# Edges of the passes in a four-layer graph kernel: split last loads, moved fills and table loads, another order at the end

## Chip, cores and metric

The kernel runs on one core of one Trainium2 chip. The metric is device time in microseconds (us) of one execution; the profile comes from one execution, and other executions were timed as well.

## What is computed

A graph of 3327 nodes with 64 features has a sparse weighted adjacency matrix `adj` (3327 x 3327, float32). Four layers follow each other, each with a residual and a normalisation:

```python
x = _layernorm(x + _L0_gnn_ref(x, adj, L0_gnn_W), axis=-1)
x = _layernorm(x + _L1_gnn_ref(L1_gnn_t, x, adj), axis=-1)
x = _layernorm(x + _L2_gnn_ref(x, adj, L2_gnn_weight, L2_gnn_bias), axis=-1)
x = _layernorm(x + _L3_gnn_ref(x, L3_gnn_W, ..., adj), axis=-1)
```

Layer 0 is two hops, `x = tanh([adj @ x, x] @ W[k])`. Layer 1 needs one product `adj @ x`. Layer 2 weights each row's neighbours by powers of 0.5 of their rank. Layer 3 runs twice what follows (H is `adj`):

```python
edge_feat = H.T @ V
att = jax.nn.softmax(Q @ edge_feat.T * scale * H, axis=1)
att_scores = att.mean(axis=0)
importance = 0.5 * structural + 0.5 * att_scores
comp_mask = jax.nn.softmax(importance / TAU) >= th_comp
cos = xn @ xn.T
edge_mask = (jax.nn.softmax(cos * H / TAU, axis=1) >= th_edge) & comp_mask[:, None]
H_pruned = H * edge_mask
...
agg = (H_pruned.T * dv_isqrt) @ transformed * de_inv[:, None]
msg = (dv_isqrt[:, None] * (H_pruned @ agg)) @ Theta
return jax.nn.relu(msg)
```

## The kernel before, in words

The matrix is padded to 3328 = 26 blocks of 128 rows (`NB` is 26, `NP` 3328, `HALF` 1664, `BANK` 512). A block is one load of 128 x 3328 float32 (1664 KB); the matrix doesn't fit on the chip, so each of 15 passes over it streams blocks from memory: `hop0`, `hop1`, `ode` (the first two layers), `decay0`, `decay1` (the third), and twice `edge`, `att`, `cos`, `down`, `up` (the fourth layer; the digit behind a name is the repetition `it`). All loads are issued by SP in one order written out by hand; each waits until the block that used its slot before is done (`block_done`).

The streams of the engines are also written by hand. What the change and the prediction touch:

- **hop, edge, down, up** (`aggregate`, `gather`): for a block, TensorE multiplies 64 feature columns by the block's two halves in chunks of 512, 512, 512 and 128 columns, into four banks of PSUM. The block's matmuls start when the whole block has landed (`landed`). In `down` and `up` VectorE first masks the block in place; it masks the last block of `up` in two parts (L1693), columns 0 to 1024 of each half and then the rest.
- **start**: SP loads the constants and the early weights (`early_constants`, L481 and L482) between the second and third block of `hop0`. After `hop0` the parts of its result are copied from PSUM (L1064 on ScalarE, L1289 on VectorE) and multiplied by those weights in `early_fold`.
- **att, cos** (`product`): TensorE makes the block of products in four pieces, VectorE multiplies each by the block of H and takes the maximum (L1480), ScalarE takes the exponential (L1188), and TensorE adds up columns with `columns(k)`, two blocks later. In `att` VectorE makes the reciprocal of the row sum (`weigh`, L1582), and for the last block multiplies it by `real`, which is 0 for the one row past 3327 (L1586). In `cos` GpSimd computes the cut of each row (`cut_of`, L608), ScalarE marks what lies below it (`sign`, L1204), VectorE prunes (L1637; the last two blocks L1642) and GpSimd prunes a share of the columns (`prune_share`, L618 and L621).
- **between the passes of layer 3**: the column sums are copied from PSUM (L1198 and L1591 after `att`, L1224 after `cos`) and turned by transposes (`turn_sums`, L933). Two softmaxes over the nodes use all-reduces of GpSimd (`node_softmax`, L626 and L628; L636 and L642 are all-reduces whose result isn't used).
- **fills**: `keep_running(n)` issues n matmuls on zeros, 512 columns each, whose result isn't used.
- **end**: after `up1` the result is folded in three parts of 8, 8 and 10 blocks of 64 columns (0, 1, 2). `kept_part`, `var_of` and `inverse_of` on VectorE, squares and roots on ScalarE, make the normalisation. ScalarE scales parts 0 and 1 a block at a time (L1264, L1270), VectorE part 2 (L1763). SP stores parts 0, 1 and 2 in that order (L572).

## Time and profile before

| what | value |
|---|---|
| timed executions, median of 3 | 1688.93 us (1687.36 to 1691.55) |
| the profiled execution, its own time | 1691.28 us |
| its span, first to last instruction | 1689.3 us |
| PE busy | 1468.6 us, 87% |
| DVE busy | 1140.3 us, 67% |
| ACT busy | 731.2 us, 43% |
| POOL busy | 348.9 us, 21% |
| DMA, mean over the span | 342 GB/s |
| chain that ended last | PE 55%, DMA 17%, DVE 16%, issue 8%, ACT 3% |

PE is TensorE's matmuls, PEld its weight loads, DVE VectorE, ACT ScalarE, POOL GpSimd, SP the queue that issues the loads. The chain that ended last is followed back from the last instruction, at each step to what released it; "issue" is time in which the engine waited for nothing that the profile shows. The clock that the profile gives is the one granted to TensorE, as a share of 2.4 GHz. A row of a timeline has the start, the duration, the engine, the line, the operation, out<-in and the count, and in brackets how long the engine had been idle and what ended that.

### The profile page before, as it was taken

Reading aid. Unit: us, or ns where it says so; the run is one execution under the profiler, and the core shown is the slowest. Engines: PE = TensorE matmul, PEld = TensorE weight load, DVE = VectorE, ACT = ScalarE, POOL = GpSimd, SP = SyncE. Lnnn points to the kernel's source line nnn. Section 1 sums busy time; section 2 is a strip of 40 time slices with the busy share of each in tenths; the row PEclk is TensorE's granted clock in tenths of the full one; section 3 lists DMA queues with packets and bytes.
Section 4 is the critical chain, followed back from the end, with each engine's and each line's share of the span. In section 5 each row is a group of like instructions: output and inputs, shape, how many; then the busy total and the mean of one; then the engine's idle time right before and its main releaser. Section 6 shows DMA issues by size and latency. Waiting matters only on the chain.

```text
span 1689.3 us, 24305 instructions
## 1 busy us (share of the span) xinstructions
PE 1468.6 (87%) x10171; PEld 632.4 (37%) x10171; DVE 1140.3 (67%) x1616; ACT 731.2 (43%) x671; POOL 348.9 (21%) x303
## 2 busy tenths in 40 slices
PE   6789999999999998676788799998996777798895
PEld 2234434434444343233332344443443333333442
DVE  0000213677612997899989798216996999989896
ACT  0000101533311775999930242113775999800433
POOL 0000000000000894444400000002992444200000
PEclk9999999999999999899999999999999999899998
DMA  9979598799799996466689999999993766699994
GB/s 401 427 297 403 220 425 335 259 319 410 303 423 383 427 425 268 167 247 247 231 332 428 419 417 426 425 426 421 413 407 119 256 243 243 243 406 427 426 424 176
DMA packets 60620, 578.41 MB, mean 342 GB/s; under 512 B 6240, under 2 KB 6496, under 8 KB 20832
## 3 DMA queue, kind: packets, MB, share of 16 engines
q1 hardware_dynamic: 60512, 576.87, 84.7%
q8 instruction: 80, 1.31, 0.3%
q14 instruction: 28, 0.23, 0.0%
HBM read 575.14 MB, written 1.70 MB: 341 GB/s over the span
## 4 chain that ended last, share of the span: by engine, by line
PE 55%; DMA 17%; DVE 16%; issue 8%; ACT 3%; SPq 0%; DVEq 0%; POOL 0%; ACTq 0%; POOLq 0%
PE ps L654 53%; DMA arena<-adj_t 8%; DMA slot<-adj 6%; DVE shared L1480 4%; DVE slot L1673 4%; DVE slot L1696 2%; DMA shared<-adj_t 2%; DVE shared L1673 2%; DMA slot<-adj_t 2%; PE ps L1008 1%; DVE shared L1696 1%; ACT shared L1234 1%; ACT shared L1188 1%; DVE slot L1637 1%; DVE slot L1642 0%
## 5 line engine op out<-in xcount | busy, mean ns | idle before, releaser
L654 PE MATMUL ps<-shared 64*128 64x416 f32 (+3 forms) x1292 | 279.4, 473 | 102.7 <-DVE max L1480 100.1
L1480 DVE CUSTOM_DVE_ANT_1 shared<-ps,slot 128x832 f32<-128x832 f32 x352 | 342.0, 1021 | 5.1 <-PE ps L654 2.5
L1188 ACT ACTIVATE shared<-shared,negmax 128x3327 f32<-128x3327 f32 x88 | 270.0, 3069 | 67.7 <-DVE negmax L1491 65.1
L654 PE MATMUL ps<-slot,cur 128*64 128x512 f32 (+1 forms) x1440 | 262.9, 516 | 16.8 <-DVE slot L1673 14.8
L593 POOL TENSOR_SCALAR cur<-shared,row_rz 128x768 f32<-128x768 f32 x32 | 70.5, 2204 | 870.7 <-DVE row_rz L1582 865.9
L654 PE MATMUL ps<-arena 64*128 64x416 f32 (+1 forms) x1072 | 208.2, 525 | 1.0 <-DMA arena<-adj 0.5
L654 PEld LDWEIGHTS ps<-shared 64*128 64x128 f32 (+2 forms) x1292 | 113.5, 162 | 235.7 <-DVE max L1480 145.5
L1234 ACT ACTIVATE shared<-ps 128x2048 int16<-128x2048 int16 (+1 forms) x52 | 78.1, 1554 | 279.5 <-PE ps L1008 279.5
L654 PEld LDWEIGHTS ps<-slot,cur 128*64 128x64 f32 x1440 | 96.7, 137 | 179.4 <-issue 154.7
L1204 ACT ACTIVATE arena<-shared,cut 128x3328 fp8e4<-128x3328 f32 x52 | 159.1, 3059 | 8.7 <-POOL cut L608 7.5
L1637 DVE SCALAR_TENSOR_TENSOR slot<-arena,slot 128x2752 f32<-128x2752 int8 x48 | 145.0, 3021 | 12.4 <-ACT arena L1204 12.4
L654 PE MATMUL ps<-shared,cur 128*64 128x512 f32 (+1 forms) x672 | 125.7, 522 | 15.1 <-DVE shared L1673 7.5
L1289 DVE COPY shared<-ps 128x512 f32<-128x512 f32 x3 | 2.1, 692 | 193.5 <-PE ps L654 193.5
L654 PEld LDWEIGHTS ps<-arena 64*128 64x128 f32 (+1 forms) x1072 | 87.6, 175 | 108.5 <-issue 69.5
L1696 DVE SCALAR_TENSOR_TENSOR slot<-shared,slot 128x3328 f32<-128x3328 int8 x32 | 114.5, 3620 | 10.7 <-ACT shared L1234 8.5
L654 PE MATMUL ps<-slot,ones 128*32 128x128 f32 (+3 forms) x1456 | 102.2, 408 | 10.3 <-DVE slot L1642 10.3
L654 PE MATMUL ps<-shared,arena 128*64 128x320 bf16 (+4 forms) x798 | 105.5, 361 | 0.4 <-DMA shared<-adj 0.4
L654 PE MATMUL ps<-slot,arena 128*64 128x512 f32 x496 | 91.0, 515 | 5.0 <-DMA slot<-adj 5.0
L1130 ACT ACTIVATE shared<-ps 128x512 int16<-128x512 f32 x104 | 53.6, 517 | 88.6 <-PE ps L654 88.3
L1064 ACT ACTIVATE shared<-ps 128x640 f32<-128x640 f32 (+1 forms) x6 | 3.9, 650 | 198.7 <-PE ps L654 198.7
L1673 DVE SCALAR_TENSOR_TENSOR slot<-arena,slot 128x3328 f32<-128x3328 int8 x24 | 85.9, 3621 | 3.0 <-DMA slot<-adj 3.0
L618 POOL TENSOR_SCALAR share_marks<-shared,cut 128x576 bf16<-128x576 f32 x48 | 82.4, 1717 | 4.7
(203 smaller groups left out, 1590.8 us busy)
## 6 DMA issues: line engine op xcount, KB each, us to landing
slot<-adj SPq DMA_DIRECT2D x159, 1664.0 KB, 9.5
slot<-adj_t SPq DMA_DIRECT2D x62, 1664.0 KB, 14.2
arena<-adj_t SPq DMA_DIRECT2D x26, 1664.0 KB, 23.9
arena<-adj_t SPq DMA_DIRECT2D x52, 832.0 KB, 7.2
shared<-adj SPq DMA_DIRECT2D x26, 1664.0 KB, 14.6
shared<-adj_t SPq DMA_DIRECT2D x22, 1664.0 KB, 15.0
arena<-adj SPq DMA_DIRECT2D x15, 1664.0 KB, 15.3
xw<-x_nodes SPq DMA_DIRECT2D x1, 832.0 KB, 4.5
```

Of the source, the lines that this page charges most:

```text
L593: weighted = pool.tensor_scalar(halves(dst), product, row_rz[:, k % 3:k % 3 + 1], None, ALU.mult)
L618: pool.tensor_scalar(marks, product, cut[:, k % 2:k % 2 + 1], None, ALU.is_ge)\
L654: return pe.matmul(o, l, r, start=start, stop=stop, skip_group_check=True)
L1008: last = pe.transpose(ps[:, 4 * BANK + q * D:4 * BANK + (q + 1) * D].bitcast(BF16), sign_pairs[:, q * HALF + pair * P:q * HALF + (pair + 1 ...
L1130: act.activation(dst, bank(c, w), ACT.Relu).then_inc(relu_act, 1)
L1188: act.activation(bufs[b][:, 0:N], bufs[b][:, 0:N], ACT.Exp, bias=negmax[:, b:b + 1], accum_out=rowsum[:, b:b + 1]).then_inc(exp_done, 1)
L1204: act.activation(interleaved(sign_marks[:, row * NP:(row + 1) * NP]), halves(prod[k % 2][:, 0:NP]), ACT.Sign, bias=cut[:, k % 2:k % 2 + 1] ...
L1234: act.activation(turned[pair % 2][:, cols], ps[:, 4 * BANK:4 * BANK + HALF].bitcast(I16)[:, cols], ACT.Copy)\
L1480: dve.tensor_tensor_reduce(out=pieces3(bufs[k % len(bufs)], c), in0=pieces_psum(piece_place(name, k, c)[0]), in1=pieces3(slot_of(name, k), ...
L1637: dve.scalar_tensor_tensor(out=own, in0=marks, scalar=0.0, in1=own, op0=ALU.is_le, op1=ALU.mult, accum_out=conn).then_inc(pruned, 1)
L1673: dve.scalar_tensor_tensor(out=slot, in0=interleaved(signs[:, row * NP:(row + 1) * NP]), scalar=0.0, in1=slot, op0=ALU.is_le, op1=ALU.mult ...
L1696: dve.scalar_tensor_tensor(out=slot, in0=marks, scalar=0.0, in1=slot, op0=ALU.is_le, op1=ALU.mult).then_inc(up_pruned, 1)
```

## The change

It has seven parts.

1. The early weights are loaded behind the last block of `hop0` instead of ahead of its third, under a semaphore of their own. VectorE's scaling of `decay_w` moves behind its copy of `hop0`'s result.
2. The last blocks of `hop0`, `edge0`, `up0`, `edge1` and `up1` are loaded in two parts. For `hop0` these are columns 512 to 1664 of each half, then 0 to 512; for the others 0 to 1024, then the rest. TensorE (`hop0`, `edge`) or VectorE (`up`) starts on the first part.
3. GpSimd runs a one-element `tensor_scalar` right behind the softmax that follows `att`.
4. The last block of `att` is summed over 127 rows of the 128, so the multiplication by `real` goes. Its sums of the first bank are made first; ScalarE copies them and TensorE turns them while those of the second bank are made and copied.
5. Ahead of `cos`'s last `columns` there are 8 fills.
6. ScalarE takes a square root that isn't used, behind its copy of `cos`'s sums.
7. At the end the order changes: part 2 is centred later, its squares are taken before part 0 is scaled, parts 1 and 2 are both scaled by VectorE, and SP stores parts 1, 2, 0.

```diff
@@ sync
+                    if name == "hop0" and k == NB - 1:
+                        for cols, signal in ((slice(BANK, HALF), first_landed), (slice(0, BANK), loaded)):
+                            sp.dma_start(halves(slot[:, :])[:, :, cols], halves(adj_t[row * P:(row + 1) * P, :])[:, :, cols])\
+                                .then_inc(signal, 16)
...
+                    if name in SPLIT_LOADS and k == NB - 1:
+                        whole = halves(source[row * P:(row + 1) * P, :])
+                        for cols, signal in ((slice(0, 2 * BANK), first_landed), (slice(2 * BANK, HALF), loaded)):
+                            sp.dma_start(halves(slot[:, :])[:, :, cols], whole[:, :, cols]).then_inc(signal, 16)
...
             early_stream("hop0")
+            sp.dma_start(early_wt, early_weights).then_inc(weights_loaded, 16)
             late_constants()
...
-            for c in range(3):
-                sp.wait_ge(out_ready, PARTS[c].stop if c < 2 else PARTS[1].stop + 1)
+            for c in (1, 2, 0):
+                if c == 0:
+                    sp.wait_ge(out_ready, PARTS[0].stop)
+                else:
+                    sp.wait_ge(ends_scaled, c)
@@ gpsimd
                 node_softmax(2 * it)
+                pool.tensor_scalar(tiny["unused_step"][:, :], ones32[:, 0:1], 1.0, None, ALU.mult).then_inc(steps_ready, 1)
@@ tensor
             def gather(name, k, source, slot):
...
+                    elif name.startswith("edge") and k == NB - 1 and o == 2 * BANK:
+                        landed(pe, name, k)
...
+                    rows_in = N - (NB - 1) * P if sums and k == NB - 1 else P
+                    chunks = sum_chunks(not sums or k >= ADDED)
+                    if sums and k == NB - 1:
+                        chunks.sort(key=lambda chunk: chunk[3] >= BANK)
+                    for i, (r, o, w, at) in enumerate(chunks):
+                        last = mm(ps[32 * r:32 * r + m, 6 * BANK + at:6 * BANK + at + w], s[0:rows_in, :],
+                                  moving[0:rows_in, o:o + w], start=False)
+                        if sums and k == NB - 1 and at < BANK <= chunks[i + 1][3]:
+                            last.then_inc(colsum_first, 1)
...
+                else:
+                    keep_running(8)
                 columns(NB - 1)
...
+                if sums:
+                    pe.wait_ge(colsum_first_sbuf, it + 1)
...
+                    if sums and t == BANK // P:
+                        pe.wait_ge(colsum_sbuf, 2 * it + 1)
@@ scalar
-                act.wait_ge(colsum_psum, 2 * it + 1)
-                act.activation(col_rows[:, 0:BANK], bank(6), ACT.Copy).then_inc(colsum_sbuf, 1)
+                act.wait_ge(colsum_first, it + 1)
+                act.activation(col_rows[:, 0:BANK], bank(6), ACT.Copy).then_inc(colsum_first_sbuf, 1)
...
+                act.activation(tiny["unused_root"][:, :], eps_t[:, :], ACT.Sqrt).then_inc(root_loaded, 1)
...
                     end_root(0)
+                    square_part(EARLY_LNS + 4, 2)
                     act.wait_ge(end_bias, 1)
+                    scaled(blocks_of(0)[:3])
                     end_root(1)
+                    scaled(blocks_of(0)[3:5])
                     end_root(2)
+                    scaled(blocks_of(0)[5:])
@@ vector
-                    if k == NB - 1:
-                        link(weight)
-                        weight = dve.tensor_tensor(row_rz[:, k % 3:k % 3 + 1], row_rz[:, k % 3:k % 3 + 1],
-                                                   real[:, k:k + 1], ALU.mult)
...
+            def out_part(c):
+                link(inverse_of(c))
+                dve.tensor_tensor(of_part(cur[:, :], c), of_part(scr_a, c), part_spread(small["var"][:, :], c), ALU.mult)\
+                    .then_inc(ends_scaled, 1)
```

`scaled(blocks)` is the loop of L1264 over some blocks of part 0.

How GpSimd's instructions stand at the start of `cos0`. `ISA` is here both an all-reduce (with its tile) and, bare, an instruction that stands before the first operation of another kind. Before:

```order
L636 ISA
L636 ISA unused<-ones 128x1
L626 ISA gmax<-pmax 128x1 [waits part_max]
L628 ISA gsum<-psum_ 128x1 [waits part_sum]
L604 MEMSET shared 128x1 [waits piece_read]
L608 ISA
L608 TENSOR_SCALAR cut<-rowsum,blocked 128x1 [waits exp_done]
```

And now:

```order
L665 ISA
L665 ISA unused<-ones 128x1
L655 ISA gmax<-pmax 128x1 [waits part_max]
L657 ISA gsum<-psum_ 128x1 [waits part_sum]
L668 ISA
L668 TENSOR_SCALAR unused_step<-ones 128x1
L633 MEMSET shared 128x1 [waits piece_read]
L637 TENSOR_SCALAR cut<-rowsum,blocked 128x1 [waits exp_done]
```

The bare `ISA` that stood behind the memset of the first block now stands behind the second all-reduce, with the new operation.

TensorE at the end of `cos0`, from the sums of the last block to the first block of `down0` (`slot,ones` are column sums, `ones_b,zeros_b` fills). Before:

```order
L654 MATMUL ps<-slot,ones 32x384 [waits pruned,piece_read]
L654 MATMUL ps<-slot,ones 32x384 x3
L654 MATMUL ps<-slot,ones 32x256 x4
L654 MATMUL ps<-slot,ones 32x128 x5
L654 MATMUL ps<-slot,ones 32x127
L654 MATMUL ps<-ones_b,zeros_b 128x1
L654 MATMUL ps<-ones_b,zeros_b 128x512 x6
L654 MATMUL ps<-slot,cur 64x512 [waits pruned,down_ready]
```

And now:

```order
L685 MATMUL ps<-ones_b,zeros_b 128x512 [waits piece_read]
L685 MATMUL ps<-ones_b,zeros_b 128x512 x7
L685 MATMUL ps<-slot,ones 32x384 [waits pruned]
L685 MATMUL ps<-slot,ones 32x384 x3
L685 MATMUL ps<-slot,ones 32x256 x4
L685 MATMUL ps<-slot,ones 32x128 x5
L685 MATMUL ps<-slot,ones 32x127
L685 MATMUL ps<-ones_b,zeros_b 128x1
L685 MATMUL ps<-ones_b,zeros_b 128x512 x6
L685 MATMUL ps<-slot,cur 64x512 [waits pruned,down_ready]
```

Eight fills stand between the sums of the last block but one and those of the last.

VectorE at the end of the program, from the last reduction of the folded result. Before:

```order
L1728 TENSOR_REDUCE mean<-arena 128x10 [waits dve_chain]
L1732 SCALAR_TENSOR_TENSOR arena<-mean,arena 128x640 [waits dve_chain]
L1743 SCALAR_TENSOR_TENSOR conn<-conn,rnorm 128x8 [waits end_squares]
L1750 RECIPROCAL var<-var 128x8 [waits part_sd]
L1758 TENSOR_TENSOR imp<-imp,var 128x8 [waits dve_chain]
L1741 TENSOR_REDUCE conn<-arena 128x8 [waits part_squared]
L1743 SCALAR_TENSOR_TENSOR conn<-conn,rnorm 128x8 [waits dve_chain]
L1750 RECIPROCAL var<-var 128x8 [waits part_sd]
L1741 TENSOR_REDUCE conn<-arena 128x10 [waits part_squared]
L1743 SCALAR_TENSOR_TENSOR conn<-conn,rnorm 128x10 [waits dve_chain]
L1750 RECIPROCAL var<-var 128x10 [waits part_sd]
L1763 TENSOR_TENSOR cur<-arena,var 128x640 [waits dve_chain]
```

And now, behind the same reduction:

```order
L1805 SCALAR_TENSOR_TENSOR conn<-conn,rnorm 128x8 [waits end_squares,dve_chain]
L1799 SCALAR_TENSOR_TENSOR arena<-mean,arena 128x640
L1812 RECIPROCAL var<-var 128x8 [waits part_sd]
L1833 TENSOR_TENSOR imp<-imp,var 128x8 [waits dve_chain]
L1817 TENSOR_REDUCE conn<-arena 128x8 [waits part_squared]
L1805 SCALAR_TENSOR_TENSOR conn<-conn,rnorm 128x8 [waits dve_chain]
L1817 TENSOR_REDUCE conn<-arena 128x10 [waits part_squared]
L1805 SCALAR_TENSOR_TENSOR conn<-conn,rnorm 128x10 [waits dve_chain]
L1812 RECIPROCAL var<-var 128x8 [waits part_sd]
L1822 TENSOR_TENSOR cur<-arena,var 128x512 [waits dve_chain]
L1812 RECIPROCAL var<-var 128x10 [waits part_sd]
L1822 TENSOR_TENSOR cur<-arena,var 128x640 [waits dve_chain]
```

Both reductions of squares now come before either reciprocal of parts 1 and 2, and the scaling of part 1 (128x512) has come over from ScalarE.

## Rows read from the trace of the kernel before

**Rows 1.** The chain that ended last, in order of time: start, us, what.

```profile
919.78 21.08 DMA slot<-adj
```

**Rows 2.** Timeline at the end of `hop0`: the last block, then the fold.

```profile
111.67 3.02 PE L654 MATMUL ps<-arena,xw 128*64 128x512 f32 x16 [0.99 <-DMA arena<-adj_t]
...
114.61 0.49 PE L654 MATMUL ps<-shared 128*128 128x128 f32 x2
```

**Rows 3.** Timeline at the end of `edge1`: TensorE, the last block.

```profile
1154.81 3.02 PE L654 MATMUL ps<-slot,arena 128*64 128x512 f32 x16 [0.97 <-DMA slot<-adj]
```

**Rows 4.** Timeline at the end of `up1`: the last block, masked and multiplied.

```profile
1665.12 3.69 DVE L1693 SCALAR_TENSOR_TENSOR slot<-shared,slot 128x2048 f32<-128x2048 int8 x2 [0.32 <-DMA slot<-adj_t]
1668.35 2.96 PE L654 MATMUL ps<-slot,cur 128*64 128x512 f32 x16
```

**Rows 5.** Timeline at the start of `cos0`: GpSimd and the first exponential's last row.

```profile
663.57 0.38 POOL L628 PARTITION_ALL_REDUCE gsum<-psum_  x1 [0.72 <-ACT node_e L1195]
...
671.24 0.10 POOL L604 MEMSET shared<- 128x1 f32 x1 [7.29 <-DVE max L1480]
...
674.44 0.19 ACT L1188 ACTIVATION_READ_ACCUMULATOR shared<-shared,negmax 128x1 f32 x1
...
678.32 0.26 POOL L608 TENSOR_SCALAR cut<-rowsum,blocked 128x1 f32<-128x1 f32 x1 [6.98 <-issue]
```

**Rows 6.** The same at the start of `cos1`.

```profile
1289.67 0.19 ACT L1188 ACTIVATION_READ_ACCUMULATOR shared<-shared,negmax 128x1 f32 x1
1293.04 0.26 POOL L608 TENSOR_SCALAR cut<-rowsum,blocked 128x1 f32<-128x1 f32 x1 [6.75 <-issue]
```

**Rows 7.** Windows: stretch, us, PE, PEld, DVE, ACT, POOL busy, PEclk, DMA share, GB/s.

```profile
690.00:840.00 150.00, 110.21 (x950) 50.44 (x952) 149.27 (x238) 147.02 (x110) 72.92 (x87) 0.98 0.70 251
```

**Rows 8.** Timeline at the end of `att0`.

```profile
657.88 0.16 DVE L1586 TENSOR_TENSOR row_rz<-row_rz,cst 128x1 f32<-128x1 f32 x1
...
659.70 0.85 PE L654 MATMUL ps<-ones_b,zeros_b 128*128 128x1 bf16 x4
659.92 0.60 ACT L1198 ACTIVATE shared<-ps 128x512 f32<-128x512 f32 x1 [2.27 <-PE ps L654]
```

**Rows 9.** Timeline at the end of `cos0`: last sums, then `down0`'s first blocks.

```profile
846.16 1.71 PE L654 MATMUL ps<-slot,ones 128*32 128x384 f32 x28
...
851.96 1.98 PE L654 MATMUL ps<-slot,ones 128*32 128x384 f32 x28 [4.09 <-DVE slot L1642]
...
855.85 3.20 PE L654 MATMUL ps<-slot,ones 128*32 128x384 f32 x28 [1.92 <-DVE slot L1642]
...
859.22 1.96 DVE L1667 TENSOR_TENSOR cur<-xw,imp 128x256 f32<-128x256 f32 x2
860.92 11.39 PE L654 MATMUL ps<-slot,cur 128*64 128x512 f32 x64
```

**Rows 10.** Windows of one us there (columns as in rows 7).

```profile
853.00:854.00 1.00, 0.94 (x20) 0.42 (x8) 1.00 (x1) 1.00 (x1) 0.00 (x0) 0.63 0.97 413
...
860.00:861.00 1.00, 1.00 (x7) 0.28 (x6) 1.00 (x1) 0.13 (x1) 0.00 (x0) 0.96 0.97 386
```

**Rows 11.** Timeline of the last 12 us.

```profile
1677.63 0.82 DVE L1728 TENSOR_REDUCE mean<-arena 128x10 f32<-128x640 f32 x1
1678.16 1.28 ACT L1249 ACT_TABLE_LOAD   x1
...
1680.01 0.68 DVE L1741 TENSOR_REDUCE conn<-arena 128x8 f32<-128x512 f32 x1
1680.13 2.76 ACT L1264 ACTIVATE cur<-arena,imp,var 128x64 f32<-128x64 f32 x8 [0.47 <-DVE imp L1758]
...
1682.91 4.17 SPq L572 DMA_DIRECT2D out<-cur  x3
1683.02 0.20 DVE L1750 RECIPROCAL var<-var 128x8 f32<-128x8 f32 x1 [2.13 <-ACT var L1249]
...
1685.90 0.83 DVE L1763 TENSOR_TENSOR cur<-arena,var 128x640 f32<-128x640 f32 x1
```

94 lines of the change are left out of this document (60 added, 34 removed).

## The prediction

> **What bounds the kernel now.** I read the chain that ended last first, then the timelines where it passes from one pass to the next. The kernel changes its bound by stage. `hop0` is bound by its loads: TensorE waits 0.99 us for its last block with the queue full [rows 2]. `att` is bound by TensorE and VectorE. In `cos` VectorE is busy 149.3 of 150 us and ScalarE 147.0, while the loads take 0.70 of the DMA engines [rows 7]. From `down` to the end of `edge1`, and again in `down1` and `up1`, the loads are the bound: a block issued at 919.78 us lands 21 us later, behind five others [rows 1]. So a saving counts if it lies at an edge, where every engine waits for one chain, and is lost if it only shortens work beside a full queue. I take the seven parts in that light.
>
> **1. Early weights.** In `hop0` a block comes every 4.01 us (3.02 of matmuls, 0.99 of waiting [rows 2]) for 1664 KB. The 320 KB that stood ahead (128 x 640 float32) cost 320/1664 x 4.01 = **0.77 us**. They now land behind the last block, 0.77 us after it, at about the old 111.7 us; the fold that needs them would start at 112.9 (below), and the cover is 1.2 us. Were the weights late, all of this term could go.
>
> **2. Split last loads.** A block's matmuls last 3.02 us. The last one of `hop0` starts 0.99 us after TensorE fell idle [rows 2], that of `edge1` 0.97 us [rows 3]. With the first part landed early (31% of a load, 1.2 us, in `hop0`; 38%, 1.5 us, in `edge1`) TensorE goes on without that gap, and what is left to do when the rest lands is more than the wait for it. Gain 0.98 + 0.97 = **1.95 us**. More is not to be had, since TensorE itself is then full. In `edge0` TensorE never waits for a load: 0. In `up1` VectorE's mask starts 0.32 us after the one before [rows 4], but its first part (about 2048/3328 of 3.69, 2.3 us) is done at 1667.4 and TensorE takes the block at 1668.35 only, directly behind the one before: 0. `up0` looks the same. Bounds: 0, if both halves land together, and 1.95 with 0.5 more where a quicker start helps `up1`.
>
> **3. GpSimd's first cut.** Of the terms this is the largest. The exponential of `cos0`'s first block ends at 674.63, but the cut that needs it starts at 678.32, 6.98 us after the memset of 671.24 to 671.34 [rows 5]. The bracket says that the 6.98 us are not a wait for another engine. In `cos1` the exponential ends at 1289.86 and the cut starts at 1293.04, 6.75 us after a memset [rows 6]. The instruction order shows a bare `ISA` between memset and cut, and none in later blocks. I read this as GpSimd changing the code that it holds, 6.8 to 7.0 us. Moved behind the all-reduce that ends at 663.95, it would be over at 670.9, and the new operation of some 0.26 us at 671.2, 3.4 us ahead of the exponential's end. The memset of the first block then comes at its old time within 0.2 us. Gain: 678.32 - 674.63 = 3.69 and 1293.04 - 1289.86 = 3.18, less 0.1 each for the hand-over, **6.7 us**. VectorE idles in front of its first prune until ScalarE's mark, so the whole pass moves. It isn't bound by loads [rows 7], and the loads of `down` begin when its blocks are freed, so nothing swallows it.
>
> GPSIMD Engine Reference in the Trainium skill (2.1 Instruction dispatch) says that the first call of newly loaded code pays about 6 us, 5.95 measured, with no instruction visible. The trace has 6.98 and 6.75 and so decides; with 5.95 only about 4.7 of the 6.7 us would have been there to win.
>
> **4. End of `att`.** The multiplication (0.16 us and its hand-over, 0.20) goes in front of the last sums [rows 8]. The early copy of the first bank wins little more: the fills behind the sums occupy TensorE until 659.70 + 0.85 = 660.55, and ScalarE's copy ended at 660.52 [rows 8]. Both limits lie together, and the fills stay. 0.2 us, twice: **0.4 us**. With the fills' end overstated it would be 0.4 each; it is 0 if 127 rows are slower than 128.
>
> **5. Eight fills in `cos`.** TensorE idled 1.92 us before the last sums, which then took 3.20 us [rows 9] instead of the 1.71 that the same 28 matmuls took two blocks earlier, since the granted clock had fallen to the 1.2 GHz level in the us from 853 and came back in that from 860 [rows 10]. `down0` started at 860.92, though VectorE's first product was ready at about 859.6 [rows 9]. With fills TensorE is busy without a break from the sums before, at 851.96. Before, it was so from 855.85 and the clock came back 4.2 us later; 4.2 us after 852 is 856.2. The fills then end at about 856.9, the sums at 858.6, seven more small fills at 860.1. Gain 0.8, at most 1.3. The four slots that `down` waits for come free that much sooner and the full queue behind it moves. I take 0.7 each, **1.4 us**. If the clock stays low throughout, a fill costs about 0.43 (twice the 0.21 of a quarter of the 0.85 of [rows 8]), eight end at 857.4, the sums at 860.6, and the fills behind at 863.2: 2.3 us later each time.
>
> TensorE: Matmul & The Clock Gate in the Trainium skill (Part 1) says that the clock is throttled unless activity releases it. That is the case for this part. Its table of matmuls at the lower level, 427 ns for 512 columns, is also the case against it, since a fill in the way of the sums costs double. Both are in the figures above without it.
>
> **6. Root ahead of time.** The table load (1.28 us [rows 11]) moves to a place where ScalarE has nothing to do for tens of us: cost 0. Its gain is in part 7.
>
> **7. The end.** Before, VectorE's last operation ends at 1686.73 and the last of three stores is issued then [rows 11]. Now, from the end of the reduction at 1678.45: variance 0 (0.2), centring of part 2 (0.8), reciprocal and product (0.4), reduction 0.7, variance 0.2, reduction 0.8, variance 0.2, reciprocal 0.2, scaling of 512 columns 0.7, reciprocal 0.2, scaling 0.83 [rows 11]: 5.2, 1683.7. ScalarE has time beside it: squares 0.7 from 1679.4, eight blocks at 0.345 (2.76/8), two roots, done at 1683.4. The root no longer waits for a table, which without part 6 would end at 1679.44 and hold it for 0.8. Then two stores stand back to back, 0.33 more: 1684.05 against 1686.75, **2.7 us**. Bounds 2.0 and 3.1.
>
> ScalarE: Activation LUTs in the Trainium skill (What ACT_TABLE_LOAD costs) adds a drain of 1.38 us to the 1.28. The trace shows the root 0.01 us behind the load, so it isn't in the sum; with it the term would be up to 1.4 larger.
>
> **The sum.** 0.77 + 1.95 + 6.7 + 0.4 + 1.4 + 2.7 = 13.9 us. The profiled execution took 1691.28, so a like one now takes 1677.4. The median of the executions shown is 2.35 lower, 1688.93, and I forecast for it **1675.1 us**.
>
> **Rivals.** (a) *The code is changed late all the same*, because it starts only when a real operation is due, or is needed twice. For it: a bare instruction is no proof of what it does. Against: the gaps are constant from the memset, not from the exponential. Without the 6.7 us: 1681.8. (b) *The fills stay at the low clock.* For it: the clock fell here in both repetitions. Against: it came back within 4.2 us of unbroken work. 1675.1 + 1.4 + 2 x 2.3 = 1681.1. (c) *The split does nothing*: 16 engines end at different times, and smaller pieces may be slower. 1675.1 + 1.95 = 1677.1. (d) *`cos` settles in a slower rhythm.* VectorE and ScalarE are both full there [rows 7], and the first cut, 3.6 us earlier, changes how GpSimd's two share operations meet theirs. It decides from 13.9/52 = 0.27 us a block, over 52 blocks; at 0.45 a block the time is 1675.1 + 23.4 = 1698.5. Against: in the trace the rhythm is the same from the second block to the last. (e) *The clock helps more*, at the end of `cos` and of `up1`: 2 x 0.6 + 0.5 less, 1673.4.
>
> **How the numbers follow.** Forecast 0.66, (a) 0.08, (b) 0.09, (c) 0.07, (d) 0.07, (e) 0.03. A measurement of this kernel can tell about 0.3%, 5.1 us. All but (d) are faster by more than that; of (d) 0.04 lies between 0.17 and 0.37 us a block (same) and 0.03 beyond. Faster 0.93, same 0.04, slower 0.03. The range goes from 1671.5 (the upper bounds of parts 5 and 7, and 2 us of scatter) to 1682.2, which holds (a), (b) and (c).
>
> **What would show it.** In the profile after: the cut of the first block of `cos0` 0.1 us behind the exponential; no gap of 1 us before the last block of `hop0` and `edge1`; the last sums of `cos` in 1.7 us and `down` starting 0.7 to 1.3 us sooner after the last prune; 8.2 us from the end of the reduction of part 2 (L1728 before) to the end of the span, where it was 10.9. The forecast is wrong if that cut still waits 3 us, if the sums start 1.5 us late behind the fills, or if a block of `cos` takes more than it did.

## The result, and the profile after

| what | before | changed | predicted |
|---|---|---|---|
| timed executions, median of 3 | 1688.93 us | 1676.05 us (1675.23 to 1677.67) | 1675.1 us (1671.5 to 1682.2) |
| ratio, 95% interval | | 0.9923 (0.9909 to 0.9937) | |
| span of the profiled execution | 1689.3 us | 1673.4 us | |
| DVE busy | 1140.3 us | 1140.3 us | |
| chain that ended last, share of "issue" | 8% | 7% | |

The changed kernel is faster by 12.9 us in the medians (0.77%, interval 0.63 to 0.91%), as forecast, within the range. VectorE's busy time is the same to the tenth: nothing became cheaper, only waits at the edges went. The spans of the two profiled executions lie 15.9 us apart, more than the medians, because that of before (1691.28 us) lay at the long end of its runs and that after (1675.23) at the short end of its own; so the terms are read below as distances between landmarks inside one trace, and the scatter of long stretches is given where it matters.

Timeline at the end of `hop0`, changed kernel: start, duration, engine, line, operation; it answers to [rows 2].

```profile
106.58 5.87 PE L685 MATMUL ps<-arena,xw 128*64 128x512 f32 x32 [0.99 <-DMA arena<-adj_t]
...
112.38 0.49 PE L685 MATMUL ps<-shared 128*128 128x128 f32 x2
```

The last two blocks are one row, x32 with no bracket inside: the gap before the last block is gone. The fold starts at 112.38 where it started at 114.61, 2.23 us sooner; the forecast had 1.75.

The same at the end of `edge1`, and what follows in `att1` ([rows 3]).

```profile
1142.98 5.81 PE L685 MATMUL ps<-slot,arena 128*64 128x512 f32 x32 [1.00 <-DMA slot<-adj]
1148.82 1.02 ACT L1241 ACTIVATE arena<-ps 128x1024 f32<-128x1024 f32 x1 [13.46 <-PE ps L685]
...
1156.07 1.02 DVE L1543 CUSTOM_DVE_ANT_1 shared<-ps,slot 128x832 f32<-128x832 f32 x1 [0.44 <-DMA slot<-adj]
```

Here too the gap is gone, but a new bracket stands in the third row: VectorE, at the second block of `att1`, waits 0.44 us for that block's load. It had no such wait before. It isn't in every trace of a kernel with this split either: six of eleven lack it, and five have 0.44 to 0.99 us (experiment 5).

Timeline of `att0`'s end ([rows 8]).

```profile
655.84 1.68 PE L685 MATMUL ps<-shared,row_rz 127*1 127x384 f32 x28 [0.20 <-DVE row_rz L1645]
656.95 0.60 ACT L1257 ACTIVATE shared<-ps 128x512 f32<-128x512 f32 x1 [1.36 <-PE ps L685]
657.45 0.84 PE L685 MATMUL ps<-ones_b,zeros_b 128*128 128x1 bf16 x4
657.67 0.56 DVE L1648 COPY shared<-ps 128x384 f32<-128x384 f32 x1 [1.88 <-PE ps L685]
658.14 0.93 PE L988 MATMUL ps<-cst,shared 128*128 128x128 f32 x7
```

127 rows take the 1.68 us that 128 took. ScalarE's copy now lies under the sums. The first transposes start at 658.14, before VectorE's copy ends at 658.23 and directly behind the last fill: before, the turn began 2.48 us after the sums began, now 2.30.

Timeline of GpSimd and ScalarE at the start of `cos0` ([rows 5]), then of GpSimd in `cos1` ([rows 6]).

```profile
668.43 0.26 POOL L668 TENSOR_SCALAR unused_step<-ones 128x1 f32<-128x1 f32 x1 [6.96 <-issue]
668.65 0.09 POOL L633 MEMSET shared<- 128x1 f32 x1
...
671.64 0.19 ACT L1247 ACTIVATION_READ_ACCUMULATOR shared<-shared,negmax 128x1 f32 x1
671.94 0.27 POOL L637 TENSOR_SCALAR cut<-rowsum,blocked 128x1 f32<-128x1 f32 x1 [3.20 <-ACT shared L1247]
```

```profile
1278.14 0.26 POOL L668 TENSOR_SCALAR unused_step<-ones 128x1 f32<-128x1 f32 x1 [7.61 <-issue]
...
1281.00 0.27 POOL L637 TENSOR_SCALAR cut<-rowsum,blocked 128x1 f32<-128x1 f32 x1 [2.56 <-ACT shared L1247]
```

The wait called "issue" has moved with the first operation of its kind, to the one-element step. The cut now waits for ScalarE and nothing else: it starts 0.11 us behind the exponential's end (671.83) where it was 3.69, and 0.10 in `cos1` where it was 3.18. In `cos1` the wait took 7.61 us, 0.9 more than before; the spare that is left is 2.56 us.

TensorE at the end of `cos0` ([rows 9]), and windows of one us there (PE, PEld, DVE, ACT, POOL busy, granted clock, DMA share, GB/s; [rows 10]).

```profile
845.53 2.21 PE L685 MATMUL ps<-slot,ones 128*32 128x384 f32 x28 [2.60 <-DVE slot L1699]
847.67 3.03 PE L685 MATMUL ps<-ones_b,zeros_b 128*128 128x512 bf16 x8
850.63 1.71 PE L685 MATMUL ps<-slot,ones 128*32 128x384 f32 x28
852.27 1.49 PE L685 MATMUL ps<-ones_b,zeros_b 128*128 128x1 bf16 x7
853.70 2.79 PE L685 MATMUL ps<-slot,cur 128*64 128x512 f32 x12
```

```profile
848.00:849.00 1.00, 1.00 (x4) 0.38 (x3) 1.00 (x1) 0.98 (x2) 0.00 (x0) 0.50 0.82 346
850.00:851.00 1.00, 1.00 (x10) 0.27 (x12) 0.45 (x4) 0.98 (x2) 0.37 (x1) 1.00 1.01 416
```

The last prune ends at 849.27. The last sums run at the high level and take 1.71 us, but they start 1.36 us after the prune, behind fills of which most ran at the low one (0.50, 1.2 GHz). From the prune's end to `down0` it is 4.43 us (5.23 before), in `cos1` 4.10 (5.10 before). That looks like the forecast's 0.8 each; experiments 3, 9 and 10 say that it isn't.

Timeline of the last 8 us ([rows 11]).

```profile
1664.49 0.82 DVE L1791 TENSOR_REDUCE mean<-arena 128x10 f32<-128x640 f32 x1
...
1665.55 0.21 ACT L1309 ACTIVATE var<-conn 128x8 f32<-128x8 f32 x1 [0.56 <-DVE conn L1805]
...
1668.44 0.69 DVE L1822 TENSOR_TENSOR cur<-arena,var 128x512 f32<-128x512 f32 x1
...
1669.15 1.81 SPq L601 DMA_DIRECT2D out<-cur  x3
1669.29 0.83 DVE L1822 TENSOR_TENSOR cur<-arena,var 128x640 f32<-128x640 f32 x1
```

The reduction of part 2 ends at 1665.31, the span at 1673.4: 8.1 us, forecast 8.2, before 10.9. From the copy of `up1`'s result it is 15.2 us instead of 17.9.

### The profile page after: what moved, and what is told of

It reads as the page before. It is cut to its first block, busy times and chain, and to the rows that moved or that the text cites. A ratio compares the mean times of both kernels' runs of the same rounds, so it can differ in the third digit from the quotient of the medians.

```text
span 1673.4 us, 24337 instructions
## 1 busy us (share of the span) xinstructions
PE 1476.8 (88%) x10187; PEld 634.7 (38%) x10187; DVE 1140.3 (68%) x1615; ACT 729.7 (44%) x665; POOL 349.3 (21%) x305
## 4 chain that ended last, share of the span: by engine, by line
PE 56%; DMA 18%; DVE 16%; issue 7%; ACT 2%; SPq 0%; POOL 0%; DVEq 0%; POOLq 0%; ACTq 0%
PE ps L685 54%; DMA arena<-adj_t 9%; DMA slot<-adj 5%; DVE slot L1730 4%; DVE shared L1543 4%; DVE slot L1759 2%; DMA shared<-adj_t 2%; DVE shared L1730 2%; DMA slot<-adj_t 2%; DMA arena<-adj 1%; PE ps L1067 1%; DVE shared L1759 1%; ACT shared L1294 1%; ACT shared L1247 1%; DVE slot L1699 0%
## 5 line engine op out<-in xcount | busy, mean ns | idle before, releaser
L685 PE MATMUL ps<-slot,ones 128*32 128x128 f32 (+3 forms) x1456 | 106.3, 422 | 6.7 <-DVE slot L1699 6.7
## 6 DMA issues: line engine op xcount, KB each, us to landing
shared<-adj SPq DMA_DIRECT2D x26, 1664.0 KB, 13.9
```

The lines of the kernel that those rows point to most:

```text
L685: return pe.matmul(o, l, r, start=start, stop=stop, skip_group_check=True)
```

## The experiments

Theory: the change's worth is the sum of the forecast's parts, with GpSimd's first cut half of it. Rivals: the cut's gain belongs to something else; the fills do nothing or stand in the way; the split is given back. Every kernel was profiled, and the table's distances are from those traces.

| kernel | fold after `hop0` | att0, last exp. to pmax | exp. to cut, cos0 / cos1 | last prune to down, 0 / 1 | edge1's last but one block to att1's last exp. | up1's copy to the end |
|---|---|---|---|---|---|---|
| before | 114.61 | 4.55 | 3.69 / 3.18 | 5.23 / 5.10 | 122.08 | 17.94 |
| changed | 112.38 | 4.11 | 0.11 / 0.10 | 4.43 / 4.10 | 121.67 | 15.18 |
| 1 step alone | 114.51 | 4.55 | 0.11 / 0.10 | 5.11 / 4.02 | 122.27 | 17.96 |
| 2 no step | 112.59 | 4.12 | 3.94 / 3.40 | 5.38 / 4.07 | 121.68 | 15.21 |
| 3 no fills ahead | 112.62 | 4.12 | 0.11 / 0.10 | 4.17 / 4.01 | 121.17 | 15.25 |
| 4 short tail | 112.61 | 4.11 | 0.11 / 0.10 | 4.99 / 4.01 | 121.18 | 15.22 |
| 5 edge1 whole | 112.59 | 4.12 | 0.10 / 0.11 | 4.21 / 4.22 | 122.38 | 15.18 |
| 6 two splits | 112.24 | 4.12 | 0.11 / 0.11 | 5.24 / 4.28 | 122.23 | 15.19 |
| 7 no root | 112.77 | 4.12 | 0.10 / 0.11 | 4.15 / 4.43 | 121.31 | 15.57 |
| 8 old end | 113.00 | 4.12 | 0.11 / 0.11 | 5.47 / 4.21 | 121.45 | 17.92 |
| 9 one fill | 112.70 | 4.12 | 0.10 / 0.10 | 4.00 / 4.00 | 121.73 | 15.25 |
| 10 changed again | 112.70 | 4.12 | 0.11 / 0.10 | 4.29 / 5.14 | 122.19 | 15.26 |
| 11 weights ahead | 113.32 | 4.12 | 0.11 / 0.10 | 4.29 / 5.56 | 121.19 | 15.20 |
| 12 copies old | 112.58 | 4.36 | 0.10 / 0.11 | 5.63 / 4.12 | 121.19 | 15.21 |

The columns, in us: where the fold starts, from the start of the trace; from the last exponential of `att0` to pmax, VectorE's maximum over the nodes (L1536 before); from the end of the first exponential of `cos` to GpSimd's cut; from the end of the last prune of `cos` to `down`'s first matmul; from the start of `edge1`'s last block but one to the end of `att1`'s last exponential; from the start of VectorE's copy of `up1`'s result to the end of the span. The end of a span is given to 0.1 us, so the last column is good to 0.05.

Two long stretches show how far a whole trace can be trusted to 1 us: from `down0`'s start to the last but one block of `edge1` the fourteen took 288.05 to 291.02 us, with 289.91 before and 288.05 in kernel 1, whose streams are the same there; from `down1`'s start to the copy after `up1` 195.44 to 197.30. A term under 1 us is therefore read from its own place.

**1. The step alone.** The kernel before, with part 3 only.

```diff
                 node_softmax(2 * it)
+                pool.tensor_scalar(tiny["unused_step"][:, :], ones32[:, 0:1], 1.0, None, ALU.mult).then_inc(steps_ready, 1)
                 for k in range(SHARED):
```

> The kernel before, with only GpSimd's one-element tensor_scalar behind the softmax that follows att (part 3 alone). If GpSimd changes its code there, out of everybody's way: the cut of the first block of cos0 and of cos1 stands 0.1 us behind the exponential's end (before: 3.69 and 3.18 us behind), both passes are otherwise the same, and the time falls by 6.7 us to a ratio of 0.9960. If the gain after the change came from elsewhere, or the code is changed a second time when the cut is due: the cut stays over 3 us late and the ratio is 1.0000.

Measured: 1682.12 us, ratio 0.9957 (0.994 to 0.9973) to 1689.27, 7.2 us less. GpSimd in `cos0`:

```profile
670.59 0.26 POOL L640 TENSOR_SCALAR unused_step<-ones 128x1 f32<-128x1 f32 x1 [7.08 <-issue]
```

The cut stands 0.11 and 0.10 us behind the exponential. One one-element operation, added where GpSimd has nothing to do, takes 6.66 us (3.69 + 3.18 - 0.21) off the kernel before. Rival (a), ratio 1.0000, is out.

**2. All but the step.**

```diff
-                pool.tensor_scalar(tiny["unused_step"][:, :], ones32[:, 0:1], 1.0, None, ALU.mult).then_inc(steps_ready, 1)
```

> The changed kernel without that tensor_scalar. The rest of the change should keep its worth: against the kernel before a ratio of 0.9963 (1688.9 - 12.9 + 6.7 = 1682.7). In the trace the time from the exponential's end to the cut is 3.2 to 3.7 us again in both cos passes, and cos0's last prune ends 3.2 us after its place in the changed kernel (849.27), relative to the end of att0. If the step's worth depends on the other parts, the ratio differs from this by more than 0.001.

Measured: 1684.57 us, ratio 0.9969 (0.9957 to 0.9981), where 0.9963 was expected (0.0006 off, inside the interval). GpSimd at the start of `cos0`:

```profile
676.38 0.26 POOL L637 TENSOR_SCALAR cut<-rowsum,blocked 128x1 f32<-128x1 f32 x1 [7.23 <-issue]
```

The wait is back, 3.94 and 3.40 us behind the exponential, 0.25 and 0.22 more than before: the stretch ahead of the exponential is 0.3 us shorter (below), the wait is not. Experiments 1 and 2 settle the largest term from both sides.

**3. No fills ahead of the last sums.**

```diff
-                else:
-                    keep_running(8)
                 columns(NB - 1)
```

> The changed kernel without the 8 fills ahead of the last sums of cos (part 5 undone). If fills pay by the clock: TensorE idles 1.9 us before the last sums, these take about 3.2 us at half the clock, and from the end of the last prune to the first matmul of down it is 5.1 to 5.2 us instead of 4.43 in cos0 and 4.09 in cos1: 0.8 and 1.0 us later, in the time 1.5 us or less. If the fills themselves are in the way (in the changed kernel they end 1.3 us after the last prune), the sums start 1.3 us sooner and down starts as early as before or earlier; the time stays or falls.

Measured: 1675.67 us, ratio 0.9913 (0.9898 to 0.9928), no slower than the changed kernel. TensorE at the end of `cos0`, then of `cos1`:

```profile
851.25 2.66 PE L685 MATMUL ps<-slot,ones 128*32 128x384 f32 x28 [0.69 <-DVE slot L1697]
...
855.26 0.65 PE L685 MATMUL ps<-slot,cur 128*64 128x512 f32 x2
```

```profile
1459.12 2.51 PE L685 MATMUL ps<-slot,ones 128*32 128x384 f32 x28 [0.69 <-DVE slot L1697]
...
1462.99 0.65 PE L685 MATMUL ps<-slot,cur 128*64 128x512 f32 x2
```

Of the two cases that were expected, the second came: the fills are in the way. The sums took 2.66 and 2.51 us, not 3.2, since the clock came back inside them (0.60 in the us from 1459.98, 1.00 in the next), and `down` began 4.17 and 4.01 us after the prune, sooner than with fills. Without the fills the sums start 0.15 us behind the prune's end; with them, behind the fills.

**4. Three fills behind the last sums, not six** (the eight ahead stay).

```diff
-                keep_running(3 if sums else 6)
+                keep_running(3)
```

> The changed kernel with 3 fills behind the last sums of cos instead of 6. After the change these six end at 853.70, where down0 starts, and VectorE's first product, begun at 852.78, should be ready 0.3 us later, at 853.1. If the fills are what down waits for: down starts 0.5 us sooner in both repetitions, and the time falls by up to 1 us. If down waits for VectorE's product (the last of the pair that ends at 854.7 or another), nothing changes. If fewer fills let the clock fall again in the first blocks of down, it costs nothing there, since down waits for its loads soon.

Measured: 1675.64 us, ratio 0.9917 (0.9902 to 0.9932). TensorE at the end of `cos0`, then of `cos1`:

```profile
848.64 2.85 PE L685 MATMUL ps<-ones_b,zeros_b 128*128 128x512 bf16 x7 [0.33 <-issue]
851.42 1.71 PE L685 MATMUL ps<-slot,ones 128*32 128x384 f32 x28
...
853.83 0.65 PE L685 MATMUL ps<-slot,cur 128*64 128x512 f32 x2
```

```profile
1463.22 0.65 PE L685 MATMUL ps<-slot,cur 128*64 128x512 f32 x2 [0.29 <-DVE cur L1724]
```

In `cos1` `down` now waits 0.29 us for VectorE's product, 4.01 us after the prune: that is the floor. In `cos0` the fills ahead ran at the low clock and ended 2.58 us after the prune (848.84), so that `down` still came after 4.99.

**5. `edge1`'s last block whole.**

```diff
-                    if name in SPLIT_LOADS and k == NB - 1:
+                    if name in SPLIT_LOADS and name != "edge1" and k == NB - 1:
...
-                    if k == NB - 1:
+                    if k == NB - 1 and it == 0:
                         first_part_landed(pe, f"edge{it}")
```

> The changed kernel with the last block of edge1 loaded whole (the other four stay in two parts). If the forecast's view holds (att is bound by TensorE and VectorE, so what edge1 wins stays won): edge1 ends 1.0 us later relative to the last mask of up0, att1 takes as long as before from there, and the time rises by 1.0 us against the changed kernel. If the gain is given back because att1's second block is then waited for: edge1 ends 1.0 us later, VectorE no longer waits 0.44 us for that block, and att1 ends within 0.5 us of its old place, so that the time rises by 0.5 us or less.

Measured: 1678.43 us, ratio 0.9935 (0.992 to 0.9949). From the start of the last but one block to the end of `edge1` it is 7.00 us (7.00 and 7.02 in the other two kernels that load it whole), against 5.81 in all eleven that split it: 1.19 us. To `att1`'s last exponential it is 122.38 us, and 122.08 and 122.27 in the other two (mean 122.24); with the split it is 121.17 to 122.23, mean 121.64. So of 1.19 us some 0.6 arrives on average.

The eleven traces with the split fall into two groups. In six VectorE has no wait at `att1`'s second block, and it is 121.17 to 121.45 us (mean 121.25). Five wait there 0.44, 0.45, 0.50, 0.97 and 0.99 us, and have 121.67, 121.68, 121.73, 122.19 and 122.23: the mean of the six plus the wait, to 0.03 us. So 1.0 us arrives, less that wait. Kernel 5 has no wait either, but six traces with the split haven't, so its absence there says nothing.

The time itself rose by 2 us, more than either; intervals of 0.0015 (2.5 us) can't tell that from 0.6.

**6. Splits for `hop0` and `edge1` only.**

```diff
-SPLIT_LOADS = ["hop0", "edge0", "up0", "edge1", "up1"]
+SPLIT_LOADS = ["hop0", "edge1"]
```

(and the waits of `edge0`, `up0`, `up1` for whole blocks)

> The changed kernel with only the last blocks of hop0 and edge1 in two parts; those of edge0, up0 and up1 are loaded whole. Forecast: these three are worth 0, so nothing changes (ratio to the kernel before 0.9923 within 0.001), and edge0, up0 and up1 end where they did. Rival: the first part of up0 or up1, begun sooner, starts a chain that ends sooner; then the result copy after up1 comes 0.3 to 0.7 us later behind down1's start than in the changed kernel.

Measured: 1675.84 us, ratio 0.9917 (0.9901 to 0.9934): nothing lost. From `down1` to the copy after `up1` it took 195.44 us, the shortest of the fourteen, and from the fold to the end of `att0` 542.7 (541.6 to 544.5 in the others).

These stretches don't hold `up0`'s split, and the one that does, from `down0`'s start to `edge1`'s last block but one, was the longest of the fourteen (291.02 us; kernel 1 and the kernel before, which load `up0`'s last block whole too, took 288.05 and 289.91). A nearer mark settles it: from the start of VectorE's mask of `up0`'s last block but one to the end of TensorE's last matmul it is 9.49 us in the kernel before, in the changed one and, to 0.01, in this one, since TensorE reaches the last block directly behind the one before in all three. So the split of `up0` is worth 0.

In `edge0` the last four blocks are one row of 11.34 us without a gap in all three. For `up1` the same stretch is 9.49 us in kernels 1 and 6, which load it whole, and in seven with the split; the other five have 9.88 to 10.14, the longest of them the kernel before. The three splits are worth 0, as forecast. In this kernel the wait behind `edge1` was largest:

```profile
1158.49 1.02 DVE L1543 CUSTOM_DVE_ANT_1 shared<-ps,slot 128x832 f32<-128x832 f32 x1 [0.99 <-DMA slot<-adj]
```

**7. No root ahead of time.**

```diff
-                act.activation(tiny["unused_root"][:, :], eps_t[:, :], ACT.Sqrt).then_inc(root_loaded, 1)
```

> The changed kernel without the unused root behind cos's sums (part 6 undone). ScalarE then loads the table of the root at the end, 1.28 us. Forecast: the load ends at about the time of the first squares and holds the root of part 0 for about 0.8 us, of which the chain at the end passes on 0 to 0.8, since VectorE's later steps wait for squares and roots in turn; from the copy of up1's result to the end of the span 15.2 us become 15.2 to 16.0. If table loads were dearer than the 1.28 us that the row shows (a drain behind them), it would be over 1.5 us more.

Measured: 1678.18 us, ratio 0.9934 (0.9919 to 0.9948); from the copy to the end 15.57 us, 0.39 more than the changed kernel.

```profile
1669.02 1.28 ACT L1308 ACT_TABLE_LOAD   x1
...
1670.31 0.21 ACT L1308 ACTIVATE var<-conn 128x8 f32<-128x8 f32 x1
```

The root comes 0.79 us after its variance was ready (1669.52), and 0.39 us of that reaches the end. A second loss, of 0.27 us, stands in `cos1` and is told below.

ScalarE: Activation LUTs in the Trainium skill (What ACT_TABLE_LOAD costs) puts a drain of 1.38 us on top of 1.28. Here the root starts 0.01 us behind the load's end, the load starts 0.02 us behind the squares before it (they end at 1669.00), and the whole is worth 0.39 us; the trace doesn't show the drain.

**8. The old order at the end** (part 7 undone, the root ahead of time kept).

```diff
-            for c in (1, 2, 0):
+            for c in range(3):
...
-                    square_part(EARLY_LNS + 4, 2)
                     act.wait_ge(end_bias, 1)
...
-            out_part(1)
-            out_part(2)
```

> The changed kernel with the order of the end as before (part 7 undone; the root ahead of time stays). Forecast: the new order is worth 2.7 us less what the root alone gives, so from the copy of up1's result to the end of the span 15.2 us become 17.1 to 17.9, and the time rises by 1.9 to 2.7 us. Rival: most of the gain is the table's (0.8 us) and of the single last store; then it is under 1.5 us.

Measured: 1679.42 us, ratio 0.9938 (0.9923 to 0.9952); from the copy to the end 17.92 us, the 17.94 of before.

```profile
1668.05 0.16 DVE L1801 SCALAR_TENSOR_TENSOR conn<-conn,rnorm 128x8 f32<-128x8 f32 x1
1668.24 0.21 ACT L1306 ACTIVATE var<-conn 128x8 f32<-128x8 f32 x1 [1.29 <-DVE conn L1801]
```

With the table there ahead of time the root only waits 1.29 us for the variance, which comes behind the centring of part 2. So in the old order part 6 is worth nothing that these spans can tell (0.02 us), and part 7 without it 17.94 - 15.57 = 2.37 us. The two together give 2.76: 0.39 of it exists only because the order moved the variance forward.

**9. A version meant to beat both:** no fills ahead, one behind.

```diff
-                else:
-                    keep_running(8)
...
-                keep_running(3 if sums else 6)
+                keep_running(3 if sums else 1)
```

> A version meant to beat both: the changed kernel without the 8 fills ahead of cos's last sums, and with 1 fill behind them instead of 6. Of the 12 cos ends of kernels with the 8 fills the span from the last prune's end to down's first matmul is 4.1 to 5.5 us, of 6 without them 4.0 to 5.2 us, and none is below 4.0. Theory: VectorE's product needs 4.0 us and TensorE's queue adds the rest, by the clock's state or by the fills. At half the clock the last sums take 3.2 us and start 0.15 us after the prune, one fill and the closing matmul about 0.6 us more: 3.95 us, just inside the 4.0. So both repetitions should show 4.0 to 4.1 us whatever the clock does, 0.5 us less than the mean of the changed kernel each, 1 us less in the time (ratio 0.9915 or so). Rival: these spans are set by something else than TensorE's queue (the clock's fall is then seen in the first matmuls of down, or the all-reduces take longer), and the span stays at 4.3 or more in one of them; or down's start is not passed on, since its loads are the bound, and the time is as that of the changed kernel.

Measured: 1675.91 us, ratio 0.9914 (0.99 to 0.9927). TensorE at the end of `cos0`, then of `cos1`:

```profile
850.37 2.41 PE L685 MATMUL ps<-slot,ones 128*32 128x384 f32 x28 [0.69 <-DVE slot L1697]
852.71 0.41 PE L685 MATMUL ps<-ones_b,zeros_b 128*128 128x1 bf16 x2
854.21 6.24 PE L685 MATMUL ps<-slot,cur 128*64 128x512 f32 x34 [1.08 <-DVE cur L1722]
```

```profile
1460.08 1.71 PE L685 MATMUL ps<-slot,ones 128*32 128x384 f32 x28 [0.69 <-DVE slot L1697]
1461.72 0.42 PE L685 MATMUL ps<-ones_b,zeros_b 128*128 128x1 bf16 x2
1463.92 2.37 PE L685 MATMUL ps<-slot,cur 128*64 128x512 f32 x10 [1.78 <-DVE cur L1722]
```

Both passes reach 4.00 us, and TensorE is now idle 1.08 and 1.78 us before `down`, waiting for VectorE. The spare is what makes the place safe: had the sums of 3.20 us come here, they would have been 0.8 us longer than the 2.41 and still covered. In the time it is not to be told from the changed kernel.

**10. The changed kernel once more**, on the same chip as 9.

> The changed kernel itself once more, beside the version with one fill on the same chip: 1676 us, ratio 0.9923 within 0.001. Its two cos ends give two more samples of the span from last prune to down: if the fills held the clock, it would be 4.1 to 4.4 in both; if the clock's fall is a matter of chance there, one of them may be 5.2 to 5.5.

Measured: 1677.16 us, ratio 0.992 (0.9908 to 0.9932). From the prune to `down`: 4.29 and 5.14 us. TensorE at the end of `cos1`:

```profile
1457.96 2.76 PE L685 MATMUL ps<-ones_b,zeros_b 128*128 128x512 bf16 x8
1460.65 1.71 PE L685 MATMUL ps<-slot,ones 128*32 128x384 f32 x28
```

The same program gave 4.10 there in its first profile and 5.14 here.

**11. Early weights ahead again** (part 1 undone).

```diff
                 sp.dma_start(cst[:, :], consts).then_inc(const_loaded, 16)
+                sp.dma_start(early_wt, early_weights).then_inc(weights_loaded, 16)
...
             early_stream("hop0")
-            sp.dma_start(early_wt, early_weights).then_inc(weights_loaded, 16)
```

> The changed kernel with the early weights loaded ahead again, behind the constants (part 1 undone; hop0's last block stays in two parts). Forecast: the fold after hop0 starts 0.77 us later than in the kernels that load them behind (112.2 to 113.0 there), in the time 0.8 us more. Since hop0 gave 2.2 instead of 1.75 us, the two parts together have 0.5 us more than their sum: if it belongs to the weights, the fold comes 1.2 us later here; if to the split, 0.8 us.

Measured: 1676.74 us, ratio 0.9919 (0.9906 to 0.9933). The fold starts at 113.32, against 112.24 to 113.00 (mean 112.62) in the eleven kernels that load the weights behind: 0.70 us, forecast 0.77. The kernels that load the last block whole have 114.61 and 114.51, so the split is worth 114.56 - 113.32 = 1.24 us. One trace against a scatter of 0.76 us is thin, but the start of the last block but one, which the split doesn't touch, says the same: 107.52 to 107.66 in the three kernels with the weights ahead (mean 107.57), 106.42 to 107.18 in the eleven (mean 106.81), 0.76 us apart. From there to the fold it is 6.94 to 6.98 us with a whole block and 5.80 to 5.83 with a split one.

**12. The copies in the old order** (half of part 4 undone).

```diff
-                    if sums and k == NB - 1:
-                        chunks.sort(key=lambda chunk: chunk[3] >= BANK)
...
-                act.wait_ge(colsum_first, it + 1)
+                act.wait_ge(colsum_psum, 2 * it + 1)
```

> The changed kernel with 127 rows in att's last sums and no multiplication, but with the sums in the old order and ScalarE's copy of the first bank behind all of them (half of part 4 undone). Forecast: the copy ahead of time is worth nothing, because the fills behind the sums occupy TensorE until the copy ends, and from the last exponential of att to the maximum over the nodes it takes as long as in the changed kernel (4.11 us in att0). Rival, since 0.44 instead of 0.2 us was measured: the copy is worth 0.2 us, and that span becomes 4.3 us; the end of the program moves by 0.5 us at most.

Measured: 1676.25 us, ratio 0.9913 (0.9898 to 0.9929). From the last exponential to pmax: 4.36 us in both repetitions, between the 4.11 of the changed kernel and the 4.55 of before.

```profile
657.45 0.84 PE L685 MATMUL ps<-ones_b,zeros_b 128*128 128x1 bf16 x4
657.66 0.60 ACT L1252 ACTIVATE shared<-ps 128x512 f32<-128x512 f32 x1 [2.08 <-PE ps L685]
...
658.31 0.98 PE L983 MATMUL ps<-cst,shared 128*128 128x128 f32 x7
```

The turn starts at 658.31, 0.05 us behind the copy's end, where it starts at 658.14 in the changed kernel. The multiplication is worth 0.19 us, the early copy 0.25, each twice.

## Why the prediction was right, part by part

**Part 1, early weights (0.77).** Right: 0.70 by experiment 11. The weights came in time; VectorE scaled them at 112.25 in the changed kernel, behind its copy, and the fold started 0.13 us later.

**Part 2, split loads (0.98 + 0.97).** The step "TensorE goes on without that gap" was right, but the term was taken as the gap alone. The last two blocks take 5.80 us to the fold instead of 6.95 (114.61 - 107.66, the last but one block before starting at 107.66), and 5.81 instead of 7.00 in `edge1`: 1.15 and 1.19. A block that stands alone lasts 3.01 us, two in one go 5.81 to 5.87, so joining them saves about 0.2 us besides the gap. In `edge1` the forecast counted the whole as kept; the eleven traces with the split show 0 to 0.99 us of it turning into VectorE's wait for `att1`'s second block. The sentence "a saving counts if it lies at an edge" missed that this edge has a full DMA queue on its other side: from 1120 to 1145 us in the changed kernel the DMA engines were busy throughout, at 420 GB/s. 0.6 arrived on average. The sum of part 2, 1.24 + 0.6 = 1.8, is near the 1.95 because two errors cancel. The zeros for `edge0`, `up0` and `up1` hold.

**Part 3, GpSimd's first cut (6.7).** Right, 6.66 us, by experiments 1 and 2. The wait was constant from its start and not tied to the exponential, which was the argument against rival (a).

That the wait is a change of code is a reading. What the runs show is that it stands before the first operation of another kind, once, and goes with it.

GPSIMD Engine Reference in the Trainium skill (2.1 Instruction dispatch) gives 5.95 us for the first call of newly loaded code, with no instruction visible. In these traces the first operation of another kind waited 6.68 (kernel 1, `cos1`) to 7.67 us (kernel 9, `cos1`) in this place. That no instruction covers the time agrees; the figure is 0.7 to 1.7 us short. By the page's figure the estimate of what was there to win is 4.8 us, where the forecast had worked out 4.7.

**Part 4, end of `att` (0.2 twice).** Under-sized: 0.44 twice. The multiplication is the 0.19. What failed is "both limits lie together, and the fills stay", which gave the early copy nothing. The fills' end was read from a modelled duration: in the changed kernel they would end at 657.45 + 0.84 = 658.29, yet the transposes behind them start at 658.14, and pmax comes 0.25 us sooner. The fills' ends are modelled in the profile, so how much each took isn't shown; the 0.25 us is. The bound of 0.4 that the forecast named for the case "with the fills' end overstated" was the right number.

**Part 5, eight fills (0.7 twice).** Wrong, though its landmarks came out as forecast (0.80 and 1.00 sooner, last sums in 1.71 us). From the last prune to `down`, nine kernels with eight fills ahead and six behind took 4.79 us on average in `cos0` and 4.46 in `cos1`, 4.62 together (4.07 to 5.63, eighteen places). Three without the fills ahead took 4.61 (4.01 to 5.23, six places).

These three aren't alike: the kernel before and kernel 1 took 4.87 (four places), kernel 3 took 4.09 (two). So the fills gained 0.2 us a place against the first two and lost 0.5 against the third, and with a scatter of 1.6 us neither is shown; what falls is the forecast's fixed gain of 0.7.

The step that failed is the one that moved the clock's return forward by as much as the fills move the begin of unbroken work: one row of one execution was taken as a fixed delay. The clock falls here with and without fills, at a moment that differs between executions of one program (experiment 10). Fills at the low level cost 0.41 us each (seven in 2.85 us, `cos0` of experiment 4) and stand in the way of the sums; at the high one seven took 1.67 us (`cos1` of the same kernel) and are nearly out of the way when the prune ends. The profile of before had both places at the low level throughout the sums, and that was read as the rule: kernel 1, with the same code there, had 5.11 and 4.02. Rival (b) described the cost of the bad case rightly in kind (the sums 2.6 us late behind the fills), but how late they come differs between executions of one program.

The change also left standing what came last in front of `down0` before: the closing matmul and the six fills behind the sums:

```profile
858.99 2.01 PE L654 MATMUL ps<-ones_b,zeros_b 128*128 128x1 bf16 x7
```

They held TensorE until `down0` started at 860.92, while VectorE's first product was there at about 859.7 (an estimate: 4.0 us behind the prune, the shortest of all these distances). Sums at the low level and fills behind them make up the 1.2 us. Kernel 9 leaves out the fills ahead and five of the six behind, and has 4.00 us in both places, with TensorE idle before `down`. Why the last sums took 1.71 to 2.66 us in the four places of kernels 3 and 9, and 3.20 in three of the four of kernel 1 and the kernel before, stays open.

**Part 6, root ahead (0), part 7, the end (2.7).** Right: 2.76 together. The forecast's 0.8 for a root that must wait for its table was right as a wait (0.79), and 0.39 of it reached the end.

**What the sum lacked.** Two short waits at the start of `cos` are gone as well. In `cos0` of the kernel before and of kernel 1, VectorE's first product waited 0.43 us on "issue"; from pmax to the first exponential's end it took 12.43 us, and 12.12 or 12.13 in all twelve others. It isn't the step (kernel 2 has the gain without it) nor the fills, the early copy, the root or the end, each of which one of the twelve undoes. The two kernels with the wait still have `att`'s multiplication in VectorE's stream, the scaling of `decay_w` in its old place, and `hop0`'s last block whole; no run put one of these back alone, so this cause stays open. In `cos1` the wait stood on ScalarE. Its first exponential, kernel before:

```profile
1286.17 0.16 DVE L1491 TENSOR_REDUCE negmax<-max 128x1 f32<-128x4 f32 x1
...
1286.70 3.07 ACT L1188 ACTIVATE shared<-shared,negmax 128x3327 f32<-128x3327 f32 x1 [7.96 <-DVE negmax L1491]
```

It starts 0.53 us behind the start of the maximum, 0.25 in the changed kernel, and the same stretch takes 12.40 instead of 12.13 us. The other kernels with 12.40 or 12.41 are 1 and 7, the three that don't have the unused root in ScalarE's stream; eleven with it have 12.11 to 12.13. So some 0.3 us go with part 6 in a place where nobody looked for it. The root brings a load of its table behind `cos0`, and the load that stood in `edge1` before (at 1105.42 us) is gone, so ScalarE has as many loads up to there and one instruction more. Why that moves the exponential isn't shown.

The measured parts, in the order of the change, then the start of `cos`, then the end: 0.70 + 1.24 + 0.6 + 6.66 + 0.88 + 0.6 + 2.76 = 13.4 us, against 12.9 between the medians of the first comparison and 13.1 in the second (1690.21 - 1677.16, experiment 10). The forecast's 13.9 had 1.4 for the fills, which no run shows, and lacked 0.5 in `att` and 0.6 at the start of `cos`. That the total is right to 1 us rests on parts 3 and 7, which were right in mechanism and size, and for the rest on errors that cancel, which is luck.

Rival (d), a slower rhythm of `cos`, did not occur: from the cut to the last prune of `cos1` it is 177.31 us before and 177.62 after, 0.01 us a block.

```profile
690.00:840.00 150.00, 110.22 (x940) 50.58 (x940) 149.26 (x239) 146.90 (x110) 70.68 (x83) 0.97 0.66 239
```

The window of [rows 7] reads the same.

## What to carry to other kernels

Look for waits that the profile calls "issue" and that are constant from the instruction before, not from the producer: they belong to the engine itself, and an operation that isn't used can take them in a place where nobody waits. Price a gap removed between two blocks by the start-to-start time of the blocks, and ask what the engine meets next: here the queue took back 0 to 1 us of 1.2. A clock that falls at one place in one profile is one sample; before fills are placed against it, look at several executions, and compare with the version that leaves the engine idle and has few fills between its last needed work and the next.
